# Second attention of a two-layer kernel: float32r halves of 64 rows in place of 75 bfloat16 rows, the weighing in mid-step, and no loops

## The reference, cut to what matters

```python
B, N, _ = x.shape                     # 1, 2048, 128
H, d = (N_HEADS, D_HEAD)              # 16 heads of 8
q, k, v = ...                         # x @ W.T + b, each (B, H, N, d)
q, k = _rope(q, k)
scores = jnp.einsum('bhnd,bhmd->bhnm', q, k) / jnp.sqrt(d)
attn = jax.nn.softmax(scores, axis=-1)
out = jnp.einsum('bhnm,bhmd->bhnd', attn, v)
return out.transpose(0, 2, 1, 3).reshape(B, N, H * d) @ Wo.T + bo
```

## Time and profile before

| what | us |
|---|---|
| median of 3 runs (lowest, highest) | 1472.51 (1470.14, 1473.41) |
| the profiled execution, its own time | 1472.52 |
| its span, first to last instruction | 1470.7 |
| PE, DVE, ACT, POOL busy in the span | 1337.8, 969.7, 879.0, 172.0 |
| second attention: first row matmul at | 505.40 |
| second attention: first exponential at | 551.57 |
| second attention: last weighing begins at | 1351.39 |

### The profile page before, as it was taken

How to read it: one execution, slowest core, us unless ns; L and a number is a source line. 1 busy time by engine, 2 the same in 40 slices (tenths; PEclk the granted TensorE clock), 3 DMA queues, 4 the chain that set the end, 5 groups by cost and what they waited for, 6 DMA issues and landing times. The chain is left out here.

```text
span 1470.7 us, 25382 instructions
## 1 busy us (share of the span) xinstructions
PE 1337.8 (91%) x7972; PEld 612.8 (42%) x7972; DVE 969.7 (66%) x1769; ACT 879.0 (60%) x2377; POOL 172.0 (12%) x327
## 2 busy tenths in 40 slices
PE   4999999999797489999899989998999999999698
PEld 3777777778464112222222222222222222223466
DVE  4656665566678597888588858886878877750400
ACT  2666656667463106667567756765776676678442
POOL 3233333333302300000000000000000000001200
PEclk9999999999889558999799979998999999999799
DMA  3100000000000300000000000000000000000101
GB/s 74 62 9 9 7 6 8 2 3 1 1 1 12 114 11 1 17 14 5 18 17 1 17 18 1 17 17 18 1 17 17 11 8 17 2 1 1 49 0 29
DMA packets 21891, 23.36 MB, mean 16 GB/s; under 512 B 5640, under 2 KB 18184, under 8 KB 21522
## 3 DMA queue, kind: packets, MB, share of 16 engines
q1 hardware_dynamic: 21778, 21.94, 4.6%
HBM read 17.54 MB, written 4.19 MB: 15 GB/s over the span
## 5 line engine op out<-in xcount | busy, mean ns | idle before, releaser
L1137 ACT ACTIVATE pb<-psum 128x512 f32<-128x512 f32 x1024 | 554.4, 596 | 291.4 <-PE psum L1029 290.6
L1065 DVE TENSOR_REDUCE rowmax<-psum 128x1 f32<-128x1024 f32 x512 | 603.0, 1219 | 151.9 <-PE psum L983 151.3
L1029 PE MATMUL psum<-qf,kf 75*128 75x512 bf16 x1024 | 396.3, 395 | 15.2 <-issue 10.6
L983 PE MATMUL psum<-kf,qf 72*128 72x512 bf16 x1024 | 375.9, 409 | 30.7 <-DVE rowmax L1065 16.0
L1009 PE MATMUL psum<-pb,vx 128*32 128x512 f32 x2048 | 275.7, 616 | 0.6 <-ACT pb L1137 0.6
L1029 PEld LDWEIGHTS psum<-qf,kf 75*128 75x128 bf16 x1024 | 99.3, 98 | 392.9 <-ACT pb L1137 329.8
L499 ACT ACTIVATE pr<-psum,nmax 128x128 f32<-128x128 f32 x256 | 93.7, 366 | 116.9 <-DVE nmax L442 112.7
L983 PEld LDWEIGHTS psum<-kf,qf 72*128 72x128 bf16 x1024 | 99.8, 101 | 138.1 <-DVE rowmax L1065 62.8
L537 POOL TENSOR_TENSOR pr<-pr,rtotal 128x256 f32<-128x256 f32 (+1 forms) x256 | 110.5, 452 | 238.6 <-DVE rtotal L450 238.6
L441 DVE TENSOR_REDUCE nmax<-psum 128x2 f32<-128x256 f32 x128 | 53.8, 420 | 65.0 <-PE psum L310 59.7
L1154 POOL COPY vx<-v 128x128 f32 (+1 forms) x16 | 4.6, 293 | 720.1 <-PE psum L1009 720.1
(11 more groups left out here) (198 smaller groups left out, 1290.7 us busy)
## 6 DMA issues: line engine op xcount, KB each, us to landing
qf<-q_parts SPq DMA_DIRECT2D x48, 96.0 KB
kf<-k_parts SPq DMA_DIRECT2D x48, 96.0 KB
q_parts<-parts SPq DMA_DIRECT2D x4, 384.0 KB, 2.5
k_parts<-parts SPq DMA_DIRECT2D x4, 384.0 KB, 2.6
cos<-cos_table SPq DMA_DIRECT2D x1, 1024.0 KB, 5.1
sin<-sin_table SPq DMA_DIRECT2D x1, 1024.0 KB, 8.4
out<-x SPq DMA_DIRECT2D x1, 1024.0 KB, 5.1
w_cur<-in_L_attn_wq SPq DMA_DIRECT2D x8, 64.0 KB, 1.9
```

The source lines that it names most:

```text
L983: mm = nc.tensor.matmul(m.psum[:, M_B + (u % 2) * 2 + n % 2, :], qf[0:QROWS, b, t * P:(t + 1) * P], kf[0:QROWS, b, c * BANK:(c + 1) * BANK ...
L1029: nc.tensor.matmul(m.psum[:, bank, :], kf[:, b, t * P:(t + 1) * P], qf[:, b, c * BANK:(c + 1) * BANK], start=True, stop=True).then_inc(st_ ...
L1065: nc.vector.tensor_reduce(rowmax[:, u // 2, u % 2:u % 2 + 1], m.psum[:, M_B + (u % 2) * 2:M_B + (u % 2) * 2 + 2, :].rearrange("p b c -> p ...
L1137: nc.scalar.activation(pb[:, t % 2, c, :], m.psum[:, exp_bank(k, last)[0], :], ACT.Exp, scale=SCALE).then_inc(exp_ready, 1)
```

## The change

Six things change together.

1. `PARTS` goes from 3 to 2, and the parts are float32r. In project1_block one ACT rounding and one POOL subtraction per job are left; the DVE subtraction and the second rounding go. The parts in memory are 4 bytes wide. A head's contraction is 2 x 2 x 8 = 32 rows and 2 rows of maxima, padded with zeros to 64.
2. Even heads live in partitions 0 to 63 of `qf` and `kf`, odd heads in 64 to 127, with two slots for each. Every row and score matmul contracts 64 rows of its own half. The padding is set once by four POOL memsets (`edge_rows`), on which PE's first row matmul waits; a transfer copies zeros over a slot's rows of maxima when it is used again.
3. A step is: score, row, score, row, weighing, score, row, score, row. The tile weighed is two behind, and `pb` has three buffers.
4. Scores, turned maxima and turned sums share the banks 4, 5 and 7 in rotation, in one list of places; each waits for the reader of the place three before it (`bank_free`). This holds in the last head too. Saving the sums of a head and dividing happen in steps 1 and 2 of the next.
5. After the first head's rows and the 12 rows of the second, PE runs four float32 matmuls of 128 x 512 that nobody reads (`KICK`).
6. All hardware loops are written out, in attn0_block and experts_block too.

```diff
-PARTS = 3
+PARTS = 2
+HALFP = P // 2
@@ attn0_block, all engines; experts_block likewise @@
-            with pe.Fori(0, LAST) as r:
+            for r in range(0, LAST):
@@ project1_block @@
-        parts = sb("parts", [P, 2, PARTS, N], BF16)
+        parts = sb("parts", [P, 2, PARTS, N], F32R)
...
-                    nc.vector.tensor_tensor(rest[:, u % 2, :], rot[:, u % 2, :], parts[:, i, 0, c * BANK:(c + 1) * BANK],
-                                            ALU.subtract).then_inc(rest_ready, 1)
...
+                nc.gpsimd.tensor_tensor(parts[:, i, 1, cols], rot[:, u % 3, :], parts[:, i, 0, cols].bitcast(F32),
+                                        ALU.subtract).then_inc(low_ready, 1)
@@ attn1_block @@
-        qf = sb("qf", [KROWS, NB, N], BF16)
-        kf = sb("kf", [KROWS, NB, N], BF16)
-        pb = sb("pb", [P, 2, NC, BANK])
+        qf = sb("qf", [P, SLOTS, N], F32R)
+        kf = sb("kf", [P, SLOTS, N], F32R)
+        pb = sb("pb", [P, 3, NC, BANK])
-        M_B, E_B, A_B, T_B = 0, 4, 6, 7
+        M_B, A_B = 0, 6
+        TURNING = (4, 5, 7)
+        KICK = 4
+        def group(h):
+            return h % 2 * HALFP
+        def bank_of(place):
+            return TURNING[place % 3]
@@ PE @@
-                mm = nc.tensor.matmul(m.psum[:, M_B + (u % 2) * 2 + n % 2, :], qf[0:QROWS, b, t * P:(t + 1) * P],
-                                      kf[0:QROWS, b, c * BANK:(c + 1) * BANK], start=True, stop=True)
+                mm = nc.tensor.matmul(m.psum[:, M_B + (u % 2) * 2 + n % 2, :], qf[g0:g0 + HALFP, b, t * P:(t + 1) * P],
+                                      kf[g0:g0 + HALFP, b, c * BANK:(c + 1) * BANK], start=True, stop=True)
+            def bank_free(place):
+                if place >= 3:
+                    reader, count = read_by[place - 3]
+                    pe.wait_ge(reader, count)
+                return bank_of(place)
+            def step(s):
+                h, t = s // NT, s % NT
+                g0, b = group(h), slot(h)
+                if t == 0:
+                    pe.wait_ge(max_rows_loaded, (h + 1) * 32)
+                for c in range(NC):
+                    bank = bank_free(exp_place(s, c))
+                    nc.tensor.matmul(m.psum[:, bank, :], kf[g0:g0 + HALFP, b, t * P:(t + 1) * P],
+                                     qf[g0:g0 + HALFP, b, c * BANK:(c + 1) * BANK], start=True, stop=True).then_inc(st_ready, 1)
+                    n = UNITS + LEAD + s * NC + c
+                    if n < H1 * UNITS:
+                        rows(n // UNITS, n % UNITS)
+                    if c == 1:
+                        if s >= 2:
+                            weigh((s - 2) // NT, (s - 2) % NT)
+                        if t == 2 and h >= 1:
+                            turn_sums(h - 1)
+                        if t == NT - 3 and h + 1 < H1:
+                            turn_max(h + 1)
+            pe.wait_ge(edge_rows, 4)
+            for n in range(UNITS):
+                rows(0, n)
+            for n in range(LEAD):
+                if n == 4:
+                    turn_max(0)
+                rows(1, n)
+            for _ in range(KICK):
+                nc.tensor.matmul(m.psum[:, A_B, :], m.ident[:, :], m.xnT[:, 0:BANK], start=True, stop=True)
@@ POOL @@
+            for i, g0 in enumerate((0, HALFP)):
+                if i:
+                    pool.wait_ge(edge_rows, 2)
+                nc.gpsimd.memset(qf[g0 + QROWS:g0 + HALFP, :, :].bitcast(F32), 0.0).then_inc(edge_rows, 1)
+                pool.wait_ge(edge_rows, 2 * i + 1)
+                nc.gpsimd.memset(kf[g0 + QROWS:g0 + HALFP, :, :].bitcast(F32), 1.0).then_inc(edge_rows, 1)
```

More of the change, by code:

```diff
@@ L8 @@
 BF16 = mybir.dt.bfloat16
+F32R = mybir.dt.float32r
 U32 = mybir.dt.uint32
@@ L472, in _ @@
                 step(0, i)
-            with dve.Fori(0, LAST) as r:
+            for r in range(0, LAST):
                 for i in range(LAG, ROUND + LAG):
@@ L515, in _ @@
                 step(0, i)
-            with act.Fori(0, LAST) as r:
+            for r in range(0, LAST):
                 for i in range(LAG, ROUND + LAG):
@@ L529, in _ @@
             pool.wait_ge(zeroed, 4)
-            with pool.Fori(0, PAIRS) as p:
+            for p in range(0, PAIRS):
                 for w in range(NT):
@@ L849, in _ @@
                                         m.psum[:, 6 + c % 2, :].rearrange("p (t d) -> p t d", d=D), bv, ALU.add).then_inc(v_saved, 1)
+        @block.scalar
+        def _(act):
+            for u in range(JOBS):
+                i, c = u // NC, u % NC
+                act.wait_ge(rot_ready, u + 1)
+                nc.scalar.activation(parts[:, i, 0, c * BANK:(c + 1) * BANK], rot[:, u % 3, :], ACT.Copy).then_inc(high_ready, 1)
         @block.gpsimd
@@ L889, in attn1_block @@
     SCALE = HD1 ** -0.5
-    HALF = 2 * BANK
-    NB = 3
     with ExitStack() as ctx:
@@ L1050, in _ @@
                     turn_max(0)
-                rows(1, 1, n)
-            with pe.Fori(0, ROUNDS) as r:
-                for b in range(NB):
-                    head(r, b)
-            for h in range(ROUNDS * NB, H1):
-                head(h // NB, h % NB)
+                rows(1, n)
+            for _ in range(KICK):
+                nc.tensor.matmul(m.psum[:, A_B, :], m.ident[:, :], m.xnT[:, 0:BANK], start=True, stop=True)
+            for s in range(STEPS):
+                step(s)
+            weigh(H1 - 1, NT - 2)
@@ new lines, in _ @@
+            dve.wait_ge(nmax_zeroed, 1)
+            for v in range(HALVES):
+                reduce_rows(v)
+            save_maxima(0)
+            reduce_rows(HALVES)
+            save_turned(0)
+            for v in range(HALVES + 1, HALVES + LEAD // 2):
+                reduce_rows(v)
+            for s in range(STEPS):
+                h, t = s // NT, s % NT
+                v = HALVES + LEAD // 2 + 2 * s
+                if v < H1 * HALVES:
+                    reduce_rows(v)
+                if t == 1 and h >= 1:
+                    save_sums(h - 1)
+                if t == 2 and h >= 1:
+                    divide(h - 1)
+                if t == NT - 3 and h + 1 < H1:
+                    save_turned(h + 1)
+                if v + 1 < H1 * HALVES:
+                    reduce_rows(v + 1)
+                if t == NT - 4 and h + 1 < H1:
+                    save_maxima(h + 1)
@@ L1127, in _ @@
+            save_sums(H1 - 1)
+            divide(H1 - 1)
         @block.scalar
         def _(act):
[L1129 to L1137 removed]
@@ L1139, in _ @@
-            with act.Fori(0, ROUNDS) as r:
-                for b in range(NB):
-                    head(r * NB + b)
-            for h in range(ROUNDS * NB, H1):
-                head(h, h == H1 - 1)
+            for s in range(STEPS):
+                for c in range(NC):
+                    if c == 0 and s >= 3:
+                        act.wait_ge(av_done, s - 2)
+                    act.wait_ge(st_ready, s * NC + c + 1)
+                    nc.scalar.activation(pb[:, s % 3, c, :], m.psum[:, bank_of(exp_place(s, c)), :], ACT.Exp,
+                                         scale=SCALE).then_inc(exp_ready, 1)
@@ L1308, in _ @@
             dve.wait_ge(y_main_added, 1)
-            with dve.Fori(0, NC) as c:
+            for c in range(0, NC):
                 dve.wait_ge(y_ready, START + c + 1)
@@ L1335, in _ @@
             chunk(0, True)
-            with act.Fori(0, NC - 1) as c:
+            for c in range(0, NC - 1):
                 chunk(c + 1, False)
@@ L1373, in _ @@
             outputs(0, HT, K, 4, y_ready)
-            with pe.Fori(0, NC - 1) as r:
+            for r in range(0, NC - 1):
                 for i in range(NETS):
```

330 lines of the change are left out of this document (123 added, 207 removed).

## The result

The changed kernel took 1373.79 us in the median of 4 runs (1373.05 to 1377.55), beside 1471.72 for the kernel before in the same job. The ratio is 0.934, interval 0.9319 to 0.936. Its profiled execution took 1373.2, with a span of 1371.4 and a mean granted clock of 0.957 (before 1470.7 and 0.939).

What follows compares the result with a forecast made beforehand. PE was taken as the bound in mid-head of the second attention, 2.89 us a step. The terms summed as 1472.5 - 117.3 + 6 + 3 - 4 - 2 + 1 = 1359 us, range 1318 to 1450.

Steps and rivals of the forecast that it cites:

- The rival of half rate: Row and score matmuls: four-byte columns stream at half rate, 0.43 per matmul; time 1518, slower; chance 0.13.
- The weight load is the slow one: PE in a step: float32r loads like float32 (185 ns), 0.08 charged per exposed place; step 2.58, against 2.42 if fast.
- The ring of 2.58: Second attention's step: with three rotating banks, waits from exponential through score, weighing and third score sum to 2.58 us.
- The 255 steps, -117.3: Second attention: 657.9 plus 15.1 for same-half steps and 7.5 for turning sums, 680.5 instead of 797.8 us.
- Saving hides in DVE's spare time: Heads' ends: saving and dividing fit DVE's spare 0.22 a step; otherwise up to 1.5 us a head, 20 in all.
- KICK +6: Ahead of the first score: four float32 matmuls cost 3.4 to 6.9, less first steps at full clock; bounds +1 and +7.
- The memsets +3: Before the first row matmul: four in series take 14.7, ending at 508.1 against 505.40; bounds 0 and +4.
- project1_block -4, loops elsewhere -2: DVE loses 0.68 per job of eight, -4 (bounds -6 and 0); three attn0_block loop boundaries of 0.67 go, -2.
- The clock from KICK on: Granted clock forecast at 1.00 from KICK to the end.
- The rival that it falls in mid-attention: Second attention: clock falls as PE waits each step; 1440 in part (chance 0.11), near 1780 throughout (0.05).
- The halves in series: Second attention: the array halves don't overlap; 237 steps at 2.94, 18 at 2.58, time 1430; chance 0.10.
- the faster rival: Second attention: the weight load is fast, step 2.42 with DVE's floor at 2.36, time 1322; chance 0.08.

Runs made afterwards that it cites:

- e2: The changed kernel with all heads in one half of the array (partitions 0 to 63), two memsets instead of four: 1544.15 us, ratio 1.0523.
- e5: The changed kernel with the last head's exponentials rotating over four banks instead of three: 1367.12 us, ratio 0.9305.
- e3: The changed kernel with the weighing at the end of a step, one tile behind instead of two: 1406.09 us, ratio 0.9579.
- e6: The changed kernel without the four float32 matmuls ahead of the first score (KICK = 0): 1372.94 us, ratio 0.9341.
- e7: The changed kernel with the zeros of qf set by DVE and only the ones of kf by POOL: 1373.25 us, ratio 0.9349.
- e8: The changed kernel with the eight hardware loops in attn0_block and experts_block put back: 1376.71 us, ratio 0.9368.
- e4: The changed kernel with the weighing in bfloat16 (pb and vx): 1323.46 us, ratio 0.9002.
- e10: The changed kernel with the edits of e4 and e5 together, bfloat16 weighing and four late banks: 1317.74 us, ratio 0.8962.
- e12: e11 with the second matmul only in steps 2 to 12, plus a float32 matmul before the fourth score from three steps before the last head: 1314.88 us.
- e11: e10 with the first row matmul of every pair issued twice: 1319.64 us, ratio 0.898.
- e9: The changed kernel without KICK, float32 matmuls filling PE's wait before the first row matmul and the first row pass: 1370.16, five runs 1407.92 to 1410.99 us.

## Why the prediction came out as it did

The forecast of 1359 was 15 us low (1373.79), inside its range and with the right mechanism in the steps. What stands ahead of the first row matmul came out at the right sum by luck. By its own steps:

- **One float32r matmul at 0.22.** Right, 0.23 without a wait. The rival of half rate is out.
- **The halves overlap.** Right: 0.01 apart, and e2 without it has 3.04 a step.
- **The weight load is the slow one.** Right: 184 ns, and mid-head steps are 2.61, not 2.42. By the Trainium skill (TensorE: Matmul & The Clock Gate, Weight-path perf modes) the fast load is for types other than float32; here float32r does not have it.
- **The ring of 2.58.** Measured 2.61, and e5 shows that it is the ring. The sum is closer than its parts, which is luck. Third score to its exponential is 0.53 (forecast 0.43), exponential to second score 0.65 (0.75), second score to weighing 0.43 (0.32), weighing to third score 1.00 (1.08). The load is exposed inside the distance to the next matmul and not ahead of the first: behind the weighing from the third score to the fourth, 1002.30 to 1002.64 = 0.34, and ahead of it from the second score to the weighing, 1003.48 to 1003.91 = 0.43.
- **The 255 steps, -117.3.** This is the term that was mis-sized: -104.7. Of the 12.6 us, 0.03 in every step makes 7.7. The three same-half steps have 3.08, 3.04 and 3.01, so 1.30 above mid-head where 1.08 was forecast, 3.1 in 14 heads. They pay the exposed load at both sides of the weighing and 0.23 a matmul. Turning the sums costs 0.59 and the step before it 0.08, where 0.5 was forecast, 2.6 in 15 heads. That makes 13.4; the first three steps, 1.92, 1.91 and 3.14, give 0.9 back.
- **Saving hides in DVE's spare time.** Right in the changed kernel, where the copy ends 0.47 before the weighing that needs it. e3 shows how little it takes to lose this: with the weighing half a step earlier in PE's order it costs 1.03 a head, within the 1.5 that I gave it.
- **KICK +6.** The way from first row to first exponential grew by 8.6: KICK 5.33, and 3.3 from the row pass itself, where four row matmuls with their slow loads take 2.53 at half clock instead of DVE's 2.36, and DVE waits 0.17 for PE each time. That part was missing. What I counted for KICK, the first steps at the full clock, is worth only 2.75 (e6).
- **The memsets +3.** They ended at 501.97, and PE waited for them to the last, as said, but not until 505 to 508, for the block began 5.6 earlier (487.78 against 493.40). From there to the first row matmul it is 14.2 instead of 12.0, so +2.2. e7 shows that without the memsets the load would have held PE to 500.82 all the same, so their own price is 1.2.
- **project1_block -4, loops elsewhere -2.** The first row matmul came 3.4 earlier, forecast 3, but not by these terms. From DVE's first rotation (462.56, before 466.26) to the start of attn1_block it is 25.2 instead of 27.1, so project1_block gave 1.9 and not 4. The DVE subtraction did go, but a job still takes 2.56 (466.05 to 468.61), before 2.52: what the subtraction gave back, DVE's addition took, 1.20 instead of 0.68 (see the last section). What was gained lies behind the eight jobs, where DVE's last subtraction and its wait of 1.15 for POOL are gone. The other 3.7 lie ahead of project1_block, where only the loops differ. With the same code there the traces put the first rotation anywhere from 462.43 to 467.06, so this figure is worth little; by the medians e8 gives the loops 2.9.
- **The clock from KICK on.** Right: 1.00 from 554.4, inside KICK, to the end of the last head. The rival that it falls in mid-attention did not occur here, but it was near: it occurred in e2, e4, e10 and e12, and in e11's last head.
- **Rivals.** The halves in series are e2, at 1544 instead of the 1430 I gave them: a serial step is 3.04 instead of 2.94, and the clock took 84. The lower bound of the faster rival rested on DVE at 2.36; DVE can do 2.26. And the price of a matmul from which half rate would decide, 0.36, does not come out of the forecast's own figures: an average of 3.13 over 255 steps is reached with 0.41 (255 x (4 x 0.41 + 1.18) + 42 x 4 x 0.41 + 7.5 = 795, against 255 x 3.13 = 798).

What stays open is what decides over the clock. A PE that is busy throughout does not win it back at once (e10's last head, at 0.50 with 20.00 of 20.00 us busy; e2; e9). More work per step went with a clock of 1.00 in e11's heads up to the last; with it left out at the heads' ends, e12 lost the clock in three of them. e2 differs from the changed kernel in the half (and two memsets) and lost it for 184 us, then had it back in its third head. Each kernel has one trace, too few to name a cause.

## What to carry to other kernels

Where PE stands between two other engines, write the ring of waits down, from one instruction's end to its next start, before adding up its busy time: one more bank took 0.49 us off a step (e5) in which no engine was at its limit. Work at half of the array is free only beside work in the other half. Where the weighing stands among another engine's instructions counted at the ends of a head, where sums are saved and maxima turned (1.4 us a head in e3), rather than in the middle (0.05 a step). Before a wait is shortened, look at what would end it next (e7: 7 us expected, 1.2 there, 0.6 left at the first exponential). One trace against one trace does not tell 3 us: with the same code ahead, the first row matmul started at times 4.6 us apart. Measure a stretch from its own start, and count a filler against the steps that it is for (e6, e11).

## What the runs showed of the hardware

- A float32r matmul of 64 rows and 512 columns is one instruction, 0.23 us at full clock. Its weight load takes 184 ns, as for float32.
- In project1_block DVE's addition of two 128x512 float32 tiles takes 1.20 us beside POOL's float32r subtraction, but 0.69 in the one job where POOL had not begun. Before, the same addition took 0.68 beside POOL's bfloat16 one. So DVE's saved instruction was paid back. The rows show that the holding up goes both ways. Before, DVE's two-operand instruction starts 0.02 ahead of POOL's and keeps its 0.68, and POOL's takes 2.28; the last of POOL's, with DVE's out of the way, takes 1.15. In the changed kernel POOL's starts 0.61 ahead and keeps its 1.27, and DVE's takes 1.20. So the one that starts first keeps its time. Which started first differs along with the type that POOL writes, and no run separates the two. After:

```profile
464.00 0.69 DVE L833 TENSOR_TENSOR rot<-direct,partner 128x512 f32<-128x512 f32 x1
...
470.55 1.27 POOL L853 TENSOR_TENSOR parts<-rot,parts 128x512 fp32r<-128x512 f32 x1 [1.29 <-ACT parts L845]
471.16 1.20 DVE L833 TENSOR_TENSOR rot<-direct,partner 128x512 f32<-128x512 f32 x1
```

Before:

```profile
472.16 0.68 DVE L838 TENSOR_TENSOR rest<-rot,parts 128x512 f32<-128x512 f32 x1
472.18 2.28 POOL L857 TENSOR_TENSOR parts<-rest,parts 128x512 bf16<-128x512 f32 x1 [10.76 <-ACT parts L870]
472.75 0.68 DVE L844 TENSOR_TENSOR rot<-direct,partner 128x512 f32<-128x512 f32 x1
```

- Row maxima over two banks take 1.13 to 1.14 each in a long series at full clock (e10: seven in 8.01 us), where pairs of them took 1.18.
- The clock can stay at half with PE busy: 184.00 of 184.00 us in e2, 89.8 of the 90 us from 510 to 600 in e9.
